# Attention scores on 64-row halves of TensorE's array, for two tiles of queries at a time

## What is computed

```python
qkv = einsum('oc,bct->bot', qkv_w, group_norm(x)) + qkv_b
weight = softmax(einsum('bct,bcs->bts', q * scale, k * scale), axis=-1)
a = einsum('bts,bcs->bct', weight, v)
x = x + einsum('oc,bct->bot', proj_w, a) + proj_b
```

## Time and profile before

| | |
|---|---|
| median of 3 runs | 4348.14 us (4347.87 to 4348.57) |
| span of the profiled execution | 4346.0 us |
| around the span, by the median (4348.14 - 4346.0) | 2.1 us |
| one pass | 271.5 us, 16 of them |
| busy: TensorE, VectorE, ScalarE, GpSimd | 99%, 76%, 66%, 58% |
| granted TensorE clock, mean | 0.999 of full speed |

### The profile page before, as it was taken

One profiled execution on the slowest core, in us unless ns is written; L12 is line 12 of the kernel. 1 busy time (PEld: TensorE's weight loads), 2 busy tenths in 40 slices (PEclk: granted clock), 3 DMA queues, 4 the chain that ended last, 5 costly groups with the idle time before them and its releaser, 6 DMA issues.

```text
span 4346.0 us, 89905 instructions
## 1 busy us (share of the span) xinstructions
PE 4295.6 (99%) x26692; PEld 3736.9 (86%) x26692; DVE 3313.6 (76%) x5483; ACT 2875.3 (66%) x5317; POOL 2505.1 (58%) x2406
## 2 busy tenths in 40 slices
PE   7999999999999999999999999999999999999999
PEld 6888888888888888888888888888888888888887
DVE  5777867788687786777867778687786877868778
ACT  4757747477474775747757476574765747667476
POOL 5655556565564655656566565565655646556465
PEclk9999999999999999999999999999999999999999
DMA  3232222322223222222222222222222222223222
GB/s 87 48 96 47 71 72 48 96 47 80 64 46 96 49 78 64 56 86 49 80 71 66 81 46 80 65 66 79 48 79 64 71 71 49 79 64 82 60 49 92
DMA packets 99933, 295.61 MB, mean 68 GB/s; under 512 B 15136, under 2 KB 15264, under 8 KB 99616
## 3 DMA queue, kind: packets, MB, share of 16 engines
q1 hardware_dynamic: 99616, 291.71, 25.0%
HBM read 123.88 MB, written 33.55 MB: 36 GB/s over the span
## 4 chain that ended last, share of the span: by engine, by line
PE 95%; DVE 2%; issue 1%; POOL 1%; ACT 1%; DMA 0%; SPq 0%; DVEq 0%; ACTq 0%; POOLq 0%
PE ps_t L760 21%; PE ps_g L714 15%; PE ps_o L772 11%; PE ps_o L773 11%; PE ps_s L751 11%; PE ps_s L749 11%; PE ps_s L714 7%; PE ps_t L714 6%; PE ps_o L714 3%; POOL x_raw L389 1%; ACT probs L479 0%; DVE spread L603 0%; DVE pt_lo L569 0%; DVE work L601 0%; PE ps_t L778 0%
## 5 line engine op out<-in xcount | busy, mean ns | idle before, releaser
L383 POOL TENSOR_SCALAR probs<-probs,row_rcp 128x1024 f32<-128x1024 f32 x1024 | 1149.9, 1123 | 1375.5 <-DVE row_rcp L564 1374.0
L560 DVE TENSOR_REDUCE row_min<-ps_s 128x1 f32<-128x1024 f32 x1024 | 1250.2, 1221 | 220.5 <-PE ps_s L751 205.0
L484 ACT CAST pt_hi<-ps_t 128x512 fp32r<-128x512 f32 x2048 | 1110.6, 590 | 446.5 <-PE ps_t L760 431.7
L569 DVE TENSOR_TENSOR pt_lo<-ps_t,pt_hi 128x512 fp32r<-128x512 f32 x2048 | 1308.5, 679 | 9.5 <-ACT pt_hi L484 5.0
L479 ACT ACTIVATE probs<-ps_s,row_min 128x1024 f32<-128x1024 f32 x1024 | 1150.7, 1124 | 215.5 <-DVE row_min L560 202.5
L760 PEld LDWEIGHTS ps_t<-const_sb,probs 128*128 128x128 f32 x8192 | 944.3, 140 | 185.5 <-DVE pt_lo L569 57.0
L760 PE MATMUL ps_t<-const_sb,probs 128*128 128x128 f32 x8192 | 1085.9, 274 | 0.8
L772 PE MATMUL ps_o<-pt_hi,v_st 128*128 128x256 f32 x4096 | 1044.4, 288 | 0.0
L773 PE MATMUL ps_o<-pt_lo,v_st 128*128 128x256 f32 x4096 | 1014.8, 282 | 0.0
L751 PE MATMUL ps_s<-kl_st,q_st 128*128 128x512 f32 x2048 | 808.3, 395 | 0.0
L772 PEld LDWEIGHTS ps_o<-pt_hi,v_st 128*128 128x128 f32 x4096 | 771.6, 188 | 39.4 <-issue 12.4
(11 more groups left out here) (110 smaller groups left out, 4918.2 us busy)
## 6 DMA issues: line engine op xcount, KB each, us to landing
wqk_raw<-in_wqk SPq DMA_DIRECT2D x130, 256.0 KB, 2.7
q_st<-kh_st SPq DMA_DIRECT2D x128, 256.0 KB, 2.9
q_st<-kl_st SPq DMA_DIRECT2D x128, 256.0 KB, 3.6
kh_st<-kh_st SPq DMA_DIRECT2D x128, 256.0 KB, 2.9
kl_st<-kl_st SPq DMA_DIRECT2D x128, 256.0 KB, 3.5
x_raw<-layer_out SPq DMA_DIRECT2D x36, 512.0 KB, 5.0
wv_raw<-in_wv SPq DMA_DIRECT2D x68, 256.0 KB, 3.6
x_raw<-in_x SPq DMA_DIRECT2D x32, 512.0 KB, 5.3
```

Source lines behind the costliest of these rows:

```text
L383: nc.gpsimd.tensor_scalar(probs[m % 2][:, :], probs[m % 2][:, :], row_rcp[:, m % 4:m % 4 + 1], 1.0, ALU.mult, ALU.mult).then_inc(probs_rea ...
L484: nc.scalar.copy(pt_hi[:, m // 2 % 2, 4 * half:4 * half + 4, (m % 2) * P:(m % 2 + 1) * P], ps_t[:, half, :].rearrange("p (b t) -> p b t", ...
L560: nc.vector.tensor_reduce(row_min[:, m % 4:m % 4 + 1], ps_s[:, m % 2, :], AX.X, ALU.min).then_inc(min_ready, 1)
L569: nc.vector.tensor_tensor(pt_lo[place], ps_t[:, half, :].rearrange("p (b t) -> p b t", b=4), f32(pt_hi[place]), ALU.subtract).then_inc(lo_ ...
```

## The change

Scores. The array is used as two halves of 64 rows. The upper half (partitions 0 to 63) computes keys 0 to 511 and the lower half (64 to 127) keys 512 to 1023, each into its own bank of PSUM. For each there are three products: high Q x high K, low Q x high K, high Q x low K. So a tile takes three pairs of half-height matmuls of 512 columns. Q and K must both be in the same half of the partitions: hi_st and lo_st keep them as they were split, and DMAs fill hi_sw and lo_sw with the halves exchanged (K only for keys 0 to 511). The wait between the DMAs is gone.

Order. TensorE transposes tile m first. In even steps it then waits for the exponentials of tiles m and m + 1 and computes the scores of tiles m + 2 and m + 3 in one stretch of six pairs; odd steps have no scores. VectorE takes both minima in the even step, with the reciprocals of m + 1 and m + 2 around them, and none in the odd step. ScalarE makes the high parts of V and of the attention's result ahead of the exponential.

V's bias. It is no longer added to V but to the sum of the two halves of the output (the probabilities of a row add up to one). V's evacuation becomes a copy, and the bias one column for each 128 channels (bv_sb) in place of 512 columns in all partitions.

The core of the diff; renamed buffers and the small statistics tiles, now parts of one, are left out:

```diff
@@ storage: K and Q as they come (st) and with the two halves of the partitions exchanged (sw)
-        q_st = [sb(f"q_st{s}", [P, T], F32R) for s in range(2)]
-        kh_st = [sb(f"kh_st{s}", [P, T], F32R) for s in range(2)]
-        kl_st = [sb(f"kl_st{s}", [P, T], F32R) for s in range(2)]
+        hi_st = [sb(f"hi_st{s}", [P, T], F32R) for s in range(2)]
+        lo_st = [sb(f"lo_st{s}", [P, T], F32R) for s in range(2)]
+        hi_sw = [sb(f"hi_sw{s}", [P, T], F32R) for s in range(2)]
+        lo_sw = [sb(f"lo_sw{s}", [P, T], F32R) for s in range(2)]
@@ SP: stack
                 sp.wait_ge(qk_split, 2 * hd + 2)
-                sp.dma_start(f32(q_st[s][0:D, :]), f32(kh_st[s][0:D, :])).then_inc(q_moved, 16)
-                sp.dma_start(f32(q_st[s][D:P, :]), f32(kl_st[s][0:D, :])).then_inc(q_moved, 16)
-                sp.wait_ge(q_moved, 32 * (hd + 1))
-                sp.dma_start(f32(kh_st[s][0:D, :]), f32(kh_st[s][D:P, :])).then_inc(stacked[s], 16)
-                sp.dma_start(f32(kl_st[s][0:D, :]), f32(kl_st[s][D:P, :])).then_inc(stacked[s], 16)
+                for swapped, straight in ((hi_sw, hi_st), (lo_sw, lo_st)):
+                    sp.dma_start(f32(swapped[s][D:P, :]), f32(straight[s][0:D, :])).then_inc(stacked[s], 16)
+                    sp.dma_start(f32(swapped[s][0:D, 0:HALF]), f32(straight[s][D:P, 0:HALF])).then_inc(stacked[s], 16)
@@ ScalarE: pair_steps
+                        if j == 2 and not (last and e == 1):
+                            v_high(hd + 1, hh + 1, 1 - e, 4 * hd)
+                        if e == 1 and j in (4, 6):
+                            attn_high(pair, p, (j - 4) // 2)
                         if not (last and m + 2 >= PT_STEPS):
                             exponential(tile + m + 2, m + 2, 2 * (tile + m) + 2)
                         if j in (3, 7) and not last:
                             evac_qk(hd + 2, col + hh + 2, j // 4, g_bank, True)
-                        if j == 2 and not (last and e == 1):
-                            v_high(hd + 1, hh + 1, 1 - e, 4 * hd)
-                        if e == 1 and j in (4, 6):
-                            attn_high(pair, p, (j - 4) // 2)
@@ VectorE: add_halves, evac_v
-                nc.vector.tensor_tensor(attn[rows, cols], ps_o[rows, 0:GROUP], o_part[k % 2][rows, :],
-                                        ALU.add).then_inc(attn_ready, 1)
+                nc.vector.scalar_tensor_tensor(out=attn[rows, cols], in0=ps_o[rows, 0:GROUP],
+                                               scalar=bv_sb[rows, bass.ds(lay * KT + p, 1)], in1=o_part[k % 2][rows, :],
+                                               op0=ALU.add, op1=ALU.add).then_inc(attn_ready, 1)
-                nc.vector.tensor_tensor(v_raw[:, b, :].rearrange("p (o n) -> p o n", o=1),
-                                        v_bank[b].rearrange("p (o n) -> p o n", o=1),
-                                        bv_all[:, bass.ds(lay, 1), :], ALU.add).then_inc(v_evac, 1)
+                nc.vector.tensor_copy(v_raw[:, b, :], v_bank[b]).then_inc(v_evac, 1)
@@ VectorE: pair_steps
                     if not last and m >= 4 and m % 2 == 0:
-                        add_halves(pair, m // 2 - 2)
-                    if not (last and m + 2 >= PT_STEPS):
-                        smallest(tile + m + 2, m + 2)
+                        add_halves(pair, lay, p, m // 2 - 2)
+                    more = not (last and m + 2 >= PT_STEPS)
                     low_part(tile + m, m, 0)
+                    if m % 2 == 0:
+                        reciprocal(tile + m + 1, m + 1)
+                        if more:
+                            smallest(tile + m + 2, m + 2)
                     low_part(tile + m, m, 1)
+                    if m % 2 == 0 and more:
+                        smallest(tile + m + 3, m + 3)
+                        reciprocal(tile + m + 2, m + 2)
                     if m == PT_STEPS - 1 or last and m >= 3 and m % 2 == 1:
-                        add_halves(pair, (m - 3) // 2)
-                    if not (last and m + 2 >= PT_STEPS):
-                        reciprocal(tile + m + 2, m + 2)
+                        add_halves(pair, lay, p, (m - 3) // 2)
@@ TensorE: scores
-                j = m % NT
-                for half in range(2):
-                    cols = slice(half * HALF, (half + 1) * HALF)
-                    nc.tensor.matmul(ps_s[:, m % 2, cols], q_st[s][:, j * P:(j + 1) * P], kh_st[s][:, cols],
-                                     start=True, stop=False)
-                    mm = nc.tensor.matmul(ps_s[:, m % 2, cols], q_st[s][:, j * P:(j + 1) * P], kl_st[s][:, cols],
-                                          start=False, stop=True)
+                tile = slice((m % NT) * P, (m % NT + 1) * P)
+                top, low = slice(0, D), slice(D, P)
+                first, second = slice(0, HALF), slice(HALF, T)
+                for n, (q, k) in enumerate(((0, 0), (1, 0), (0, 1))):
+                    nc.tensor.matmul(ps_s[:, m % 2, first], (hi_st, lo_st)[q][s][top, tile],
+                                     (hi_sw, lo_sw)[k][s][top, first], start=n == 0, stop=n == 2)
+                    mm = nc.tensor.matmul(ps_s[:, m % 2, second], (hi_sw, lo_sw)[q][s][low, tile],
+                                          (hi_st, lo_st)[k][s][low, second], start=n == 0, stop=n == 2)
                 mm.then_inc(scores_ready, 1)
@@ TensorE: pair_steps
+                        transpose(tile + m, m)
                         if not (last and m + 2 >= PT_STEPS):
-                            pe.wait_ge(exp_ready, tile + m + 1)
-                            s = (m + 2) // NT % 2
-                            if j == NT - 2:
-                                pe.wait_ge(stacked[s], 32 * (4 * i + p + 1 + e))
-                            scores(m + 2, s)
+                            if m % 2 == 0:
+                                pe.wait_ge(exp_ready, tile + m + 2)
+                                s = (m + 2) // NT % 2
+                                if j == NT - 2:
+                                    pe.wait_ge(stacked[s], 64 * (4 * i + p + 1 + e))
+                                scores(m + 2, s)
+                                scores(m + 3, s)
                         elif m == PT_STEPS - 2:
                             pe.wait_ge(exp_ready, tile + m + 1)
                             project(0, 0, 3)
                         else:
                             project(0, 3, 6)
-                        transpose(tile + m, m)
```

41 lines of the change are left out of this document (20 added, 21 removed).

## The result

The changed kernel takes 4645.17 us (median of 4 runs, 4644.3 to 4646.87) against 4348.26 us before (4347.87 to 4348.57): ratio 1.0684, 95% interval 1.0669 to 1.0699. It is 297 us slower; the forecast was 168 slower, and 4645 lies outside the range of 4305 to 4600.

The account below looks back on a forecast made before the run. It took TensorE (99% busy) as the bound, with a new 6.41 us loop binding short periods; three normal pairs at +2.0, last pair +4.4 and head +0.1 gave +10.5 a pass, sixteen times +168: 4516 us, range 4305 to 4600.

Parts of the forecast that it names:

- no wait for the moves of K and Q: DMAs that move K and Q: they land in 3.6 us, steps before they are needed, so they cost 0.
- Rival 1: Steps 2 to 11: the array's gain arrives because only TensorE's branch counts; -44 us, 4304 us; chance 0.18.
- e: TensorE's cost of entering and leaving a half-height stretch: 0.29 us taken, range 0 (no drain) to 0.58 (drains).
- +10.5: Sum of the predicted extra time per pass, in us; sixteen passes give +168 us.
- steps 0-1: 6.41: First period of a pair of heads: lengthens from 4.99 to the floor of the new loop, 6.41 us.
- The loop itself, 6.41: Loop through VectorE, GpSimd, TensorE and ScalarE closed by the new order: no two-step period can be under 6.41 us.
- 7.15: Periods of steps 4-5, 8-9 and 12-13: ScalarE's lateness after evacuating Q and K makes them 7.15 us instead of 6.72.
- 6.72: Periods of steps 2-3, 6-7, 10-11: TensorE's own need, 6.89 - 0.465 + 0.29 = 6.72 us.
- 9.35: Steps 14 and 15 of a normal pair: TensorE's own work binds, 9.52 - 0.465 + 0.29 = 9.35 us.
- forecast +0.1: Head of a pass: two scores standing alone between other matmuls add 0.1 us a pass.
- The sum ... 0: VectorE's sum of halves with V's bias: covered by ScalarE's high part, so 0; without that cover, upper end 19 us.
- Each may lose up to 0.1: V's evacuation as a copy on VectorE: each of 128 may lose up to 0.1 us, with 0 effect on the time.

Follow-up runs that it names:

- run 1: The changed kernel's orders and V's bias, but with the scores and the moves of K and Q of the kernel before: 4653.7 us, ratio 1.0702.
- run 5: Changed kernel with the first evacuation of Q and K moved from step 3 to step 4, behind the half copy and high parts: 4583.2 us.
- Run 2: Half-height pairs in the old engine orders, one tile per stretch ahead of the transposes, V's bias in the sum: 4449.9 us, 1.0234 to the kernel before.
- Run 6: Changed kernel with ScalarE's last high part of a pair moved behind the first two of the next pair: 4597.6 us.
- run 3: Kernel before with only V's bias moved to the sum of the halves and V's evacuation as a copy: 4360.4 us, ratio 1.0027.
- run 12: Changed kernel with two-tile stretches ahead of the transposes, VectorE taking reciprocal(m+1) and minimum(m+2) before both low parts, minimum(m+3) and reciprocal(m+2) after: 4681.8 us.
- runs 7 and 8: Changed kernel with GpSimd's multiplication in two halves of 512 columns: 4604.7 us; with that, the later evacuation and the later attention cast together: 4508.2 us.
- run 4: Changed kernel with VectorE's reciprocal of m + 2 put ahead of the minimum of m + 3: 4701.9 us, ratio 1.0812 to the kernel before.
- run 11: Changed kernel with two-tile stretches ahead of the transposes and VectorE's reciprocal(m + 1) behind low part 0: 5238.4 us.

## Why the prediction was wrong in size

**Right.** Slower, and by the step named: the loop minimum, low part, minimum, reciprocal, multiplication, transposes, and from there by the stretch or by the high part back to the minimum. It shows as the last pair's 6.50 and as TensorE's wait for probabilities, and run 1 shows that orders and not the array make it (+306 at full height). Right, too: the halves side by side, hidden loads, the minimum 1.85 behind the stretch after an evacuation (run 5 takes it away), and no wait for the moves of K and Q.

**Rival 1** (faster below e = 0.07) fell on both conditions: e is 0.39, and VectorE's side reaches the minimum. Run 2, without that loop, is still slower.

**What failed** is the size: +18.6 a pass for +10.5. By the terms of the sum:

- "steps 0-1: 6.41" is the step that failed: 7.52, and 7.34 for the last pair's, with 7.26 in the first pair together 2 x 1.11 + 0.85 + 0.93 = 4.0 of the 8.1 missed. I counted ScalarE's lateness after the evacuations of steps 3, 7 and 11 and none across the border of two pairs; I didn't look at what closes a pair on ScalarE and stands ahead of high part 0 (half copy, wait for the sum, high part of the sum). Before, this queue had slack, and no wait row named it. Run 6 moves the one instruction and gets the 6.51 back in three of the four pairs. In the first pair it is V's high part that stands there; no run moved that one.
- The loop itself, 6.41: 6.50. The transposes' first matmul came 0.14 behind the end of the multiplication and not 0.05 (that was taken from another pair of engines), and the minimum 2.03 behind the transposes and not 1.97: high part 0 starts 0.69 behind them and not 0.64. The other branch grew to the same 2.03 with the entry into the array's other shape (the stretch is 1.02 behind the transposes). About 0.5 in the rest of the last pair.
- "7.15" after an evacuation: 7.49, 7.21, 7.23, 1.4 a pass. The next stretch comes 1.26 + 1.02 behind the start of the multiplication and not 1.17 + 0.87: there I left out the entry into the array's other shape. In steps 4-5 the split of GpSimd that I left out at 0.1 adds 0.13. In steps 8-9 the earlier minimum (1.72 and not 1.84) takes 0.12 off.
- "6.72" for a full period: 6.82, 0.9 a pass. e was 0.39 and not 0.29, a 0.10 that is a size only.
- 9.35: 9.28, 0.2 a pass the other way, but only by a misreading. The earlier trace rows calls the scores at 1027.12 and 1030.33 those of steps 13 and 14; they are those of steps 14 and 15, since the next pair begins at 1036.48. So steps 14 and 15 took 9.36 before and not 9.52, and steps 2 and 3 took 7.04 and not 6.89. The sum of a pair stays. The right term would have been 9.19, and the 9.28 is the e of 0.39 on top.
- The rest of a pass: forecast +0.1, measured 1.5. In the head the distance from tile 0's scores to tile 1's is 6.56 instead of 6.35, and from there to the first stretch of the first pair 7.43 instead of 6.35: the transposes of step 0 (0.96) now stand between them. They should come back behind the last pair, but from its first projection to the next pass's first scores it is 50.3 for 50.0 before. Why wasn't traced.
- "The sum ... 0": run 3 alone says +12 us, 0.75 a pass; how much of it acts in the changed kernel, within the terms above, no run separates. The cover that I named (the high part ahead of it on ScalarE) isn't whole: in step 4 low part 0 starts 0.78 behind the high part instead of 0.61. And in run 3 the longer sum moves the low parts, for which TensorE waited at 217 places already. The bound that I gave, 19 us, held it. "Each may lose up to 0.1" for the copy was wrong: 0.

**The cost of the change of shape.** The way in and out costs 0.36 to 0.39 us per stretch. That agrees with the Trainium skill (TensorEngine Tiling, Key Properties), by which a change of tiling mode drains TensorE: of the prediction's two values for e, the 0.58 with drains was nearer than the 0 without.

**Open.** Whether a loop through two stretches would vanish with four buffers for the probabilities and the scores' statistics wasn't tried; PSUM holds two tiles of scores. Why the periods of run 12's last pair are 7.53 to 7.62 at full clock and not 6.98, and why one period in runs 7 and 8 is 6.8, I don't know. No version was faster than the kernel before. By the distances between starts the most that the array could give is 0.075 per two tiles, 38 us, less the 12 of the bias (an estimate).

## What to carry to other kernels

Where an instruction is moved behind another on an in-order engine, write down the loop that this closes through all engines, and compare its floor with the shortest periods and with the first period behind a boundary: what closes the previous block stands in the same queues, and a trace in which it had slack names no wait for it. A change of the array's shape has to be counted with its way in and out: by 0.36 to 0.39 us per stretch, three pairs lose against four full-height matmuls, and six gain 4% of eight. And work that delays a waiting instruction may be the cover of another wait: taking it out of the loop (run 4) cost 57 us.

## What the hardware showed that I had not expected

- 64-row halves run side by side at 0.23 us a pair of 512 columns, each half's next weights loaded during its own matmul; the cost is all at the borders, where the next full-height load starts only when the stretch is over (0.36 idle ahead of it).
- A copy of 128x512 from PSUM takes 692 ns on VectorE, the addition of a second operand from SBUF 691. A scalar operand per partition made the sum of 64x256 dearer: 483 for 421.
- GpSimd's multiplication of half the columns takes 0.69 of the 1.12 of the whole.
- Behind the start of the kernel, waits of TensorE up to 1.25 us left the granted clock at 1.00 all through the changed kernel. In run 12 it fell to 0.50 for about 3 us behind 14 of 32 waits of 1.77, in run 11 behind 4 of 16; behind waits of 1.68 to 1.74 (48 in run 12, 112 in run 11) it never fell.
